# Returning expert outputs to token order: gathers after the slot stage, or indirect stores from each slot tile

## The reference, cut to what matters

```python
x = layernorm(x + attention(x))              # x: (2048, 512)
logits = x @ w_router                        # (2048, 8)
top_vals, top_idx = top_k(logits, 2)
probs = softmax(top_vals)                    # two shares for each token
y_e = square(relu(x @ w_fc[e])) @ w_proj[e]  # for the two chosen experts e
out = layernorm(x + sum over the two of probs * y_e)
```

## Time and profile before

| | us |
|---|---|
| median of 3 runs (range) | 1524.15 (1523.88 to 1527.39) |
| profiled execution | 1524.27 |
| its span in the trace | 1522.6 |
| TensorE busy | 1431.2 (94%) |
| VectorE busy | 769.3 (51%) |
| ScalarE busy | 727.5 (48%) |
| GpSimd busy | 421.6 (28%) |

### The profile page before, as it was taken

How to read it: one execution, slowest core, us unless ns; L and a number is a source line. 1 busy time by engine, 2 the same in 40 slices (tenths; PEclk the granted TensorE clock), 3 DMA queues, 4 the chain that set the end, 5 groups by cost and what they waited for, 6 DMA issues and landing times. The chain is left out here.

```text
span 1522.6 us, 26278 instructions
## 1 busy us (share of the span) xinstructions
PE 1431.2 (94%) x7936; PEld 1209.1 (79%) x7937; DVE 769.3 (51%) x1773; ACT 727.5 (48%) x1633; POOL 421.6 (28%) x413
## 2 busy tenths in 40 slices
PE   7999999999999999999999999699999679999990
PEld 5888888888888888888888887588888468887870
DVE  6555555655555555555555555345445423333333
ACT  5555555655665655656655655222222123333333
POOL 1221212212221221221212211143233433443385
PEclk9999999999999999999999999899999789999995
DMA  4111011011121111111112120745454476556499
GB/s 154 48 42 62 34 56 58 32 62 48 41 62 48 41 59 51 41 48 62 42 48 62 31 80 21 263 155 203 155 194 165 120 219 242 187 193 227 152 187 214
DMA packets 71979, 160.23 MB, mean 105 GB/s; under 512 B 14096, under 2 KB 14736, under 8 KB 69520
## 3 DMA queue, kind: packets, MB, share of 16 engines
q1 hardware_dynamic: 61168, 109.55, 22.2%
q0 software_dynamic: 10784, 50.36, 10.9%
HBM read 107.36 MB, written 52.52 MB: 105 GB/s over the span
## 5 line engine op out<-in xcount | busy, mean ns | idle before, releaser
L317 POOL TENSOR_TENSOR small<-small,half 128x4 f32<-128x4 f32 x193 | 194.6, 1008 | 761.9 <-DVE small L346 761.9
L434 DVE CUSTOM_DVE_ANT_0 logit<-score_ps,bias 128x128 f32<-128x128 f32 (+3 forms) x256 | 124.9, 488 | 156.7 <-PE score_ps L531 118.7
L269 ACT ACTIVATE prob<-logit,small 128x128 f32<-128x128 f32 (+3 forms) x256 | 144.2, 563 | 118.5 <-DVE small L434 114.6
L544 PEld LDWEIGHTS y_ps<-vs,prob_t 128*128 128x128 f32 x1280 | 174.8, 191 | 21.9 <-ACT prob_t L276 4.5
L544 PE MATMUL y_ps<-vs,prob_t 128*128 (+1 forms) x1280 | 185.0, 275 | 1.0 <-ACT prob_t L276 0.7
L276 ACT ACTIVATE prob_t<-prob_ps 128x128 f32<-128x128 f32 (+3 forms) x256 | 111.5, 436 | 53.3 <-PE prob_ps L537 52.2
L763 ACT ACTIVATE yt_hi<-turn_ps,subln 128x512 fp32r<-128x512 f32 x64 | 44.0, 688 | 170.4 <-PE turn_ps L1025 157.9
L537 PE MATMUL prob_ps<-ident,prob 128*128 128x128 f32 x640 | 112.8, 274 | 3.3 <-ACT prob L269 3.3
L1034 PE MATMUL out_ps<-w_hi,yt_hi 128*128 128x512 f32 x256 | 107.6, 421 | 6.3 <-DVE yt_lo L867 6.3
L488 PE MATMUL k_ps<-w_hi,x_hi 128*128 (+1 forms) x256 | 104.1, 407 | 5.8 <-DVE w_lo L385 5.8
L488 PE MATMUL v_ps<-w_hi,x_hi 128*128 (+1 forms) x256 | 107.0, 418 | 0.0
(11 more groups left out here) (185 smaller groups left out, 3264.3 us busy)
## 6 DMA issues: line engine op xcount, KB each, us to landing
y_scratch<-x_now SPq DMA_DIRECT2D x65, 256.0 KB, 2.9
x_raw<-in_x_t SPq DMA_DIRECT2D x64, 256.0 KB, 2.8
y_raw<-y_scratch SPq DMA_DIRECT2D x15, 1024.0 KB
w_raw<-in_w_experts POOLq DMA_DIRECT2D x7, 2048.0 KB, 8.3
w_hi<-in_w_experts POOLq DMA_DIRECT2D x7, 2048.0 KB, 8.3
w_raw<-in_w_all SPq DMA_DIRECT2D x16, 768.0 KB, 5.5
slots_y<-zeros SPq DMA_DIRECT2D x13, 768.0 KB
y_raw<-slots_x SPq DMA_DIRECT2D x39, 256.0 KB
```

What stands on the lines that cost most here:

```text
L269: nc.scalar.activation(prob[:, 0:width], logit[:, 0:width], ACT.Exp, scale=-1.0, bias=least[:, h:h + 1], accum_out=row_sum[:, (i % 2) * HG ...
L317: nc.gpsimd.tensor_tensor(r, ms, half[:, :], ALU.pow).then_inc(ready, 1)
L434: nc.vector.tensor_tensor_reduce(out=logit[:, 0:width], in0=score_ps[:, 0:width], in1=bias[:, h, T - width:T], scale=1.0, scalar=3e38, op0 ...
L544: mm = nc.tensor.matmul(y_ps[:, h * D:(h + 1) * D], prob_t[:, j * P:(j + 1) * P], one(vs[:, bass.ds(now, 1), j, h * D:(h + 1) * D]), start ...
```

## The change

Each slot now carries a note of three words: the share, the row to which its result goes, and a flag. The row is the token's number, plus 2048 if this is the slot with the larger number of the token's two; the flag is 1 in the slot with the smaller number. Unused slots point to spare rows behind these. In the slot stage VectorE adds flag times the slot's own x1 row to the result, behind ScalarE's multiplication. Results of the first 24 slot tiles are stored to `slots_y` as before, and GpSimd, once all weights are split, brings them back to SBUF (`bring`) and stores them by rows into `rows_d` (`spread_rows`). Results of the last 15 stay in SBUF (`kept`, which takes the place of `x1`) and are stored by rows from there. From slot tile 32 on, each such store waits for the one before. Then SyncE loads, for each token tile, its rows of both halves ("planes") of `rows_d`, VectorE adds them, and the rest is as before. It waits for 36 stores or the number of real tiles first, and for all 39 ahead of token tile 12.

`slots_y` is no longer cleared, `x1` and `slot` are not kept, and `pad` is gone: the whole of `slots_x` is cleared during attention, by SyncE, from a zero array in DRAM, 512 KB behind each y store and 2.3 MB once ahead of the last iteration. The rows of four slot tiles are loaded ahead, where two were. `slot_tables` stands ahead of the last `gates`.

```diff
 # attention, SyncE, per token tile, behind the y store
+    tiles = slice(n * CLEARED, (n + 1) * CLEARED) if last else bass.ds(n * CLEARED, CLEARED)
+    sp.dma_start(x_slots[:, tiles, :], zeros.unsqueeze(1).to_broadcast([P, CLEARED, C])).then_inc(cleared, 16)
...
+left = SPARE_TILE + 1 - its * TB * CLEARED
+sp.dma_start(x_slots[:, its * TB * CLEARED:, :], zeros.unsqueeze(1).to_broadcast([P, left, C])).then_inc(cleared, 16)
 # token steps
-for dst, src in zip((before, experts, run, floors, tiles), route_consts):
+for dst, src in zip((before, experts, run, floors, tiles, tokens, spare_rows), route_consts):
...
-                if s_between(s, 1, CLEAR_STEPS):
-                    sp.dma_start(dst, zeros[:, :].unsqueeze(1).to_broadcast([P, CLEARED, C])).then_inc(y_cleared, 16)
-            for e in range(EARLY_PADS):
-                pad(sp, e)
...
-                nc.scalar.activation(out, x1_now[:, b, :], ACT.Copy).then_inc(x1_kept, 1)
...
+                nc.vector.reciprocal(notes[:, b, 0, 0:1], either[:, :]).then_inc(first_share, 1)
+                nc.vector.tensor_tensor(notes[:, b, 0, 2:3], slot_f[:, 0:1], slot_f[:, 1:2], ALU.is_lt)
+                nc.vector.tensor_tensor(notes[:, b, 1, 2:3], slot_f[:, 0:1], slot_f[:, 1:2], ALU.is_gt)
+                nc.vector.tensor_tensor(notes[:, b, 1, 0:1], second[:, b:b + 1], notes[:, b, 0, 0:1], ALU.mult)
+                for j in range(2):
+                    op = nc.vector.scalar_tensor_tensor(note_bits[:, b, j, 1:2], notes[:, b, 1 - j, 2:3],
+                                                        float(NT * P), row, ALU.mult, ALU.add)
 # slot stage, SyncE: notes twice, into gs (for ScalarE and VectorE) and notes_of (for GpSimd)
+            def load_notes(k, at, y):
+                sp.dma_start(gs[:, y, :], rows_of(g_slots[bass.ds(at, 1), :, :])).then_inc(g_loaded[y], 16)
+                sp.dma_start(into, rows_of(g_slots[bass.ds(at, 1), :, :])).then_inc(g_loaded[y], 16)
 # slot stage, VectorE, last of each slot step
+            def add_kept(k, y, late):
+                dve.wait_ge(gated, k + 1)
+                row = yo_of(k, y, late)
+                nc.vector.scalar_tensor_tensor(row, xs[:, y, :], shares[:, y, 2:3], row, ALU.mult, ALU.add)
 # slot stage, GpSimd, behind the last expert's weights
-            for t in range(NT):
-                pool.indirect_dma_start(x1[:, t, :], None, slots_y, ..., compute_op=ALU.add)   # and 16 more
+            def spread_rows(k, src):
+                if k >= YB:
+                    pool.wait_ge(spread[y], k // YB * 16)
+                pool.indirect_dma_start(rows_d, bass.IndirectOffsetOnAxis(ap=notes_of[:, k, 1:2], axis=0), src, None)
+            def bring(k):
+                pool.wait_ge(yo_stored[y], k // YB * 16 + 32)
+                pool.dma_start(w_raw[:, k % RAW, :], y_slot[k]).then_inc(brought[y], 16)
+            for k in range(YB):
+                bring(k)
+            for k in range(FROM_KEPT):
+                pool.wait_ge(brought[k % YB], k // YB * 16 + 16)
+                spread_rows(k, w_raw[:, k % RAW, :])
+                if k + YB < FROM_KEPT:
+                    bring(k + YB)
+            for k in range(FROM_KEPT, SLOT_TILES):
+                pool.wait_ge(yo_ready, k + 1)
+                if k >= 2 * NT:
+                    pool.wait_ge(spread[(k - 1) % YB], (k - 1) // YB * 16 + 16)
+                spread_rows(k, kept[:, k - FROM_KEPT, :])
 # final part, SyncE
+            spread_up_to(SLOT_TILES - 3)
+            spread_up_to(sp.value_load(end_i[0:1, E - 1:E], min_val=2 * NT, max_val=SLOT_TILES))
+            for t in range(NT):
+                if t == SLOT_TILES - 3 - FROM_KEPT:
+                    spread_up_to(SLOT_TILES)
+                if t >= HB:
+                    sp.wait_ge(rows_summed, t - HB + 1)
+                for half, into in enumerate((kept[:, t, :], w_raw[:, t % RAW, :])):
+                    sp.dma_start(into, row_tiles[half, t]).then_inc(halves_loaded[t % HB], 16)
 # final part, VectorE
+                nc.vector.tensor_tensor(row, row, w_raw[:, t % RAW, :], ALU.add).then_inc(rows_summed, 1)
```

More of the change, by code:

```diff
@@ L619, in mixture_phase @@
 def mixture_phase(nc, sem, y_scratch, w_last, subln, early_loaded, wait_for_y, x_d, w_router, route_consts, w_experts,
-                   x1_now, slot_now, run_i, zeros, slots_x, slots_g, slots_y, y_cleared, out_d, tables, shared):
-    ident, w_raw, w_hi, w_lo, x1, slot, we_split, raw_loaded, dispatched, gates_sent = shared
-    end_i, n_tiles, bases, owner, from_tile, tables_known, padded, pad = tables
+                  x1_now, slot_now, slots_x, slots_g, slots_y, rows_d, cleared, out_d, tables, shared):
+    ident, w_raw, w_hi, w_lo, kept, we_split, raw_loaded, dispatched, gates_sent = shared
+    end_i, n_tiles, owner, from_tile, tables_known = tables
     ctx = ExitStack()
@@ L675, in mixture_phase @@
         either = sb("either", [P, 1])
[L676 removed]
+        notes = sb("notes", [P, 2, 2, 3])
+        note_bits = notes[:, :, :, :].bitcast(dt.uint32)
+        tokens = sb("tokens", [P, NT])
+        no_notes = sb("no_notes", [P, SPARE_TILE + 1, 3], dt.uint32)
+        spare_rows = sb("spare_rows", [P, SPARE_TILE + 1])
         def ps(name):
@@ L935, in place @@
                 nc.vector.tensor_copy(slot_now[:, b, :], slot_f[:, :]).then_inc(slots_ready, 1)
-                out = slot[:, t, :] if isinstance(t, int) else one(slot[:, bass.ds(t, 1), :])
-                nc.vector.tensor_copy(out, slot_f[:, :])
             def slot_tables():
@@ L1122, in mixture_phase @@
         yo_stored = [sem(f"yo_stored{y}") for y in range(YB)]
-        second_gathered = [sem(f"second_gathered{t}") for t in range(GB)]
-        first_gathered, end_stats_done = [sem("first_gathered0"), sem("first_gathered1")], sem("e_stats_done")
+        gated = sem("gated")
+        brought = [sem(f"brought{y}") for y in range(YB)]
+        spread = [sem(f"spread{y}") for y in range(YB)]
+        halves_loaded = [sem(f"halves_loaded{u}") for u in range(HB)]
+        rows_summed, end_stats_done = sem("rows_summed"), sem("e_stats_done")
         end_var_ready, end_var_biased, end_rstd_ready = sem("e_var_ready"), sem("e_var_biased"), sem("e_rstd_ready")
@@ L1130, in mixture_phase, with yo_of @@
         out_tiles = out_d.rearrange("(t p) c -> t p c", p=P)
+        row_tiles = rows_d[0:ROWS, :].rearrange("(j t p) c -> j t p c", j=2, p=P)
         LOOPED = (SLOT_TILES - 4) // YB
         def slot_steps(engine, slot_step):
-            with engine.Fori(0, LOOPED) as quad:
-                for y in range(YB):
-                    slot_step(quad * YB + y, y % 2, quad * 2 + y // 2, y, quad)
+            for late, first, last in ((False, 0, FROM_KEPT // YB), (True, FROM_KEPT // YB, LOOPED)):
+                with engine.Fori(first, last) as quad:
+                    for y in range(YB):
+                        slot_step(quad * YB + y, y % 2, quad * 2 + y // 2, y, quad, late)
             for k in range(YB * LOOPED, SLOT_TILES):
-                slot_step(k, k % 2, k // 2, k % YB, k // YB)
+                slot_step(k, k % 2, k // 2, k % YB, k // YB, True)
+        def yo_of(k, y, late):
+            if not late:
+                return yo[:, y, :]
+            at = k - FROM_KEPT
+            return kept[:, at, :] if isinstance(k, int) else one(kept[:, bass.ds(at, 1), :])
         def more(k, ahead):
@@ L1347, in slot_step @@
                     split_x(b, k + 3)
+                add_kept(k, y, late)
             slot_steps(dve, slot_step)
@@ L1492, in build @@
+        shared = (ident, w_raw, w_hi, w_lo, sb("kept", [P, KEPT, C]), sem("we_split"), sem("raw_loaded"),
+                  [sem("dispatched0"), sem("dispatched1")], [sem("gates_sent0"), sem("gates_sent1")])
         mixture_phase(nc, sem, y_scratch, a["w_last"], subln, early_loaded, wait_for_y, a["x"], a["w_router"],
-                      (a["before"], a["experts"], a["bases"], a["floors"], a["tiles"]), a["w_experts"],
-                      x1_now, slot_now, run_i, zeros, slots_x, slots_g, slots_y, y_cleared, out_d, tables, shared)
+                      (a["before"], a["experts"], a["bases"], a["floors"], a["tiles"], a["tokens"], a["spare_rows"]),
+                      a["w_experts"], x1_now, sb("slot_now", [P, 2, 2], dt.uint32), slots_x, slots_g, slots_y, rows_d,
+                      cleared, out_d, tables, shared)
```

251 lines of the change are left out of this document (100 added, 151 removed).

## The result

The changed kernel takes 1544.51 us (median of 4 runs, 1543.5 to 1548.39); the kernel before, run beside it, takes 1524.02. The ratio is 1.0142, with a 95% interval of 1.0129 to 1.0156: 1.4% slower, where 1557 had been forecast, within 1540 to 1583. The profiled execution has a span of 1541.7 us, against 1522.6 before.

A forecast was written before the change was run, and what follows sets the result against it. Before, TensorE bounds attention, then GpSimd, TensorE and finally the gathers pace the slot stage. GpSimd free at 1436.0, tile 35 landed 1517.2, statistics done 1549.7, plus 6.3 gives span 1556.0; plus 1.6, 1557.6, say 1557 us (1540 to 1583).

The forecast's parts named there:

- Two more constants: Kernel front: two more SyncE issues and a small copy behind the last constant, +1.2 us (0.5 to 6).
- Token steps: Attention: VectorE gets four small operations ahead of normalising and loses a copy, about 0.05 a step, +0.7 us (0 to 4).
- Transition, to the first weight load: Start of slot stage: without pad stores the first slot tile loads faster, −3 us (−5 to 0).
- Added VectorE operation: Slot stage: an added operation reading two SBUF operands per tile slows GpSimd's splits, +5 us (0 to 8).
- Doubled note loads: Slot stage: 39 more loads of 0.5 KB beside the weight loads, +1 us (0 to 4).
- (d): Rival: less slow, contention and front terms at their low ends, final stage at the loads' pace; 1541; chance 0.08.
- GpSimd's start: After the weight splits: GpSimd free at 1430.5 plus 4.9 of front terms plus 0.6 loop end, 1436.0.
- The period: GpSimd's catching up: 20 steps of indirect store (1.28) and plain load (0.93), 2.21 us each; tile 24 at 1489.0.
- The late stores: From tile 32 each store awaits the previous landing, 3.44 + 0.5 to wake; four take 15.8 us, tile 35 at 1513.8.
- The final stage: After tile 35 lands, uncovered: first loads in at 1521.7, sixteen token tiles at 1.75 us, then 6.3 to the end.
- (b): Rival: the DMA engines pace the catching up, at 197 GB/s +27 us, 1571 to 1584; chance 0.17.
- (c): Rival: not slower, GpSimd's late steps and landings cheaper, 1526 down to 1513, deciding point store 35 landing at 1486; chance 0.05.

The follow-up runs named there:

- a kernel with the same instructions: The kernel before, with slot tiles 36 to 38 computed only if in use: 1523.24 us, ratio 1.0001.
- the version of 1518: Changed kernel with results kept in SBUF, four stores per weight-load wait, spaced later stores, plane loads freed, tiles 36 to 38 only if used: 1518.11 us, ratio 0.9976.

## Why the prediction was right, step by step

| Step | Forecast | Measured |
| --- | --- | --- |
| Clears in attention | 0 (0 to 6) | +1.0 by the last y store; −0.1 to 1.0 in the twelve traces with the clears |
| Two more constants | +1.2 | +0.5 |
| Token steps | +0.7 | −0.9 |
| Transition, to the first weight load | −3 | −2.6 |
| Added VectorE operation | +5 (0 to 8) | +4.0 (2.9 to 5.1) |
| Doubled note loads | +1 | not seen: waits for w_hi 55.9 us against 60.3 |
| GpSimd starts on the loads back | 1436.0 | 1428.3 |
| Period of the catching up | 2.21 | 1.85, mean 1.89 |
| Tile 24 stored | 1489.0 | 1475.55 |
| Tiles 32 to 35, each | 3.94 | 3.46 |
| Tile 35 stored | 1513.8 | 1498.25 |
| From there to the first sum | 7.9 | 8.6 |
| A token tile in the final stage | 1.75 | 1.65 |
| Behind the last aggregate | 6.3 | 8.5 |
| Span | 1556.0 | 1541.7 |

The mechanism held: GpSimd's catching up, four stores one landing at a time, then a final stage that nothing covers. The 14.3 us between forecast and span are sizes of terms. Nearly all of them erred to the same side: the change cost 20.5 us by the medians, where 33 had been forecast. The range reached down to 1540 because of (d), whose terms weren't those that came in short; that the time lies inside it is in part luck.

**GpSimd's start, −7.7.** The sum of the front was +4.9 on a base of 1430.48. Of the 7.7 us, 4.4 are that GpSimd's waits for `w_hi` came to 55.9 us against 60.3 in the trace of before, where three of the seven were 9.1 to 10.6 us; the rest is the doubled note loads, whose cost was never there, and smaller terms. The base may simply have been late, one profiled execution taken for the kernel: a kernel with the same instructions had 1426.33, 4.2 us sooner, while seven traces with the changed kernel's front lie between 1425.95 and 1427.98. With two traces of the old front this isn't settled.

**The period, −5.8 up to tile 24.** The step "a plain DMA issue costs 0.62 + 0.31 = 0.93" failed. The 0.31 of idle time was read off ahead of an indirect store and put ahead of a plain load too. Behind a store a plain load has none: 1431.70 + 1.01 is 1432.71, and the load starts at 1432.70. With 0.55 for the load the period is 1.85. Some of the gain was lost again ahead of tile 24, where a load that hadn't landed held a store for 1.17 us, a wait that the forecast had put at nothing.

**The late stores, −2.1.** Spacing 3.46 against 3.44 + 0.5: 0.96 of issuing and 2.50 of waiting, and the half microsecond for waking was already in it. The estimate by the Trainium skill (DMA: Bandwidth & Descriptors, Anatomy of one DMA) would have made it 2.6 + 0.5 = 3.1; the measurement lies between the two. (3.4 us off the forecast's 1557.6 is 1554, and not the 1553 of the prediction.)

**The final stage, +1.3 in all.** To the first sum it took 0.7 us more, and the sixteen tiles 1.6 less: in step they take 1.52, and three waits for loads, 1.3 us in all, with smaller gaps bring the mean to 1.65. What follows the last aggregate had been got from the end of before by taking away four of eight normalisings, with 0.4 for the longer power. But in the kernel before only 0.3 us lay between the last aggregate and ScalarE's start; here variance, power and scaling take 1.6, then 2.9 for the four tiles, and 4.0 to the landing of the last output store. The forecast also had GpSimd done with its stores before the first power is wanted; the last spare tile's store, issued at 1513.81, held that power to 1514.80, with no effect on the end.

**VectorE's operation** came out at 4.0 for 5, and the run without it ties it to that operation. The Trainium skill (SBUF — State Buffer, Who interferes with whom) has GpSimd's reads and two-input VectorE operations exclude each other; the direction agrees with the 72 ns a split, and taken strictly, at 8 us, it was twice too much.

**The rivals.** (b), that the DMA engines pace the catching up, is out: at a share of 0.89 and 297 GB/s the changed kernel's period was the sum of GpSimd's instructions, and without the loads it followed them too, in two kernels. The 197 GB/s of the accumulating gathers was not a limit for plain indirect stores. (c) had named the right lever: the landing of store 35, with 1486 as the point from which the change doesn't cost (by its own sum 1484: the span of 1522.6 less the 38.8 that it put behind the landing). It landed by 1501 here, where the next store no longer waits, and by 1474.5 in the version of 1518, where SyncE's first load goes. (d) came nearest in time, though by other terms than its own: not by contention or the loads' pace, but by the issue cost of the loads and the start.

What the prediction did not have at all is ScalarE's stall. In the changed kernel it costs nothing: the idle stretch of 5.92 us from 1479.8 on falls on the spare tiles, ahead of a first sum that waits for the stores. It puts TensorE's last product at 1494.3, where 1486 to 1490 had been named as a sign. It is what makes the obvious repairs fail, one at a time.

## What to carry to other kernels

When work moves behind an engine's last duty, count that engine's instructions at their issue cost, each kind with its own gap, and look for the waits of the same engine earlier on: here four stores fitted into each weight load's wait, and the 48 us of catching up shrank to nine stores, 11 to 14 us. A repair that gives nothing may have met the next wait only, so free the next one too before dropping it. And take a base date from more than one execution where a few microseconds matter.

## What the runs showed of the hardware that was not expected

Indirect stores of 128 rows of 2 KB, issued by GpSimd every 1.26 us with 0.30 us between them, go together with a stop of ScalarE: idle stretches of 17.0, 9.9 and 8.0 us in a train of 30; 4.96 and 8.58 in one of 14; 3.0 and 3.8 in one of 9; 5.9 in the changed kernel's of 9; 7.7 in one of 12 in the run without VectorE's added operation. In the 17.0, the 4.96, the 5.9 and the 7.7 ScalarE's input came 1.6 to 2.0 us after it fell idle; for the rest of them, and for all of the 9.9, 8.0, 8.58, 3.0 and 3.8, it was there. The stop begins some five to eight stores into a train. With 0.64 us between the stores (24 of them) there was none, nor with the plain load between them (0.85), nor with at most two stores on their way. The DMA engines aren't full meanwhile: during the train of 30 they were busy 0.57 of the time. What ScalarE waits for, the traces don't show; no run tells apart a delay of its instructions from one of its semaphores, or the spacing of the stores from their number on the way.

An indirect store costs GpSimd 0.96 to 1.00 us and 0.30 of idle time ahead, a plain load of 256 KB 0.55 and no idle time behind a store. In the run with results kept in SBUF and paced by landings, GpSimd waited up to 8.1 us for the landing of a store issued behind a 2 MB load on its queue, where a store alone took 3.46 from issue to issue.
